# Token lists from one-hot products, and routed weights split one stage earlier

## The reference, cut to what matters

```python
shared_out = einsum('nh,dh->nd', silu(x_flat @ sw1.T) * (x_flat @ sw3.T), sw2)   # hidden 1024
s = sigmoid(x_flat @ router_w.T + t_bias)                    # 8 scores per token
_, topk_idx = top_k(s + router_bias, 2)                      # two experts per token
gates = s_sel / (denom + EPS)
H = gelu(einsum('nd,ehd->enh', x_flat, rw1))                 # hidden 256, every expert
O = einsum('enh,edh->end', H, rw2)
out = (shared_out + einsum('end,ne->nd', O, combine)) / 3
```

## Time and profile before

| | |
|---|---|
| median of three runs | 2856.93 us |
| the profiled execution | 2873.89 us, its span 2872.2 us |
| PE busy | 2552.8 us (89%) |
| DVE, ACT, POOL busy | 1227.9, 1012.8, 649.8 us |
| mean granted PE clock | 0.949 |
| shared stage | to about 722 us |
| routed stage | 722 to 1106 us |

### The profile page before, as it was taken

One profiled execution on the slowest core, in us unless ns is written; L12 is line 12 of the kernel. 1 busy time (PEld: TensorE's weight loads), 2 busy tenths in 40 slices (PEclk: granted clock), 3 DMA queues, 4 the chain that ended last, 5 costly groups with the idle time before them and its releaser, 6 DMA issues. The chain is left out here.

```text
span 2872.2 us, 43064 instructions
## 1 busy us (share of the span) xinstructions
PE 2552.8 (89%) x12487; PEld 2091.2 (73%) x12488; DVE 1227.9 (43%) x1642; ACT 1012.8 (35%) x1582; POOL 649.8 (23%) x572
## 2 busy tenths in 40 slices
PE   5776699999778784899899897799997999999999
PEld 1565578887666663788788786799996888888876
DVE  4412233333666663344343342566663333333346
ACT  3112233332766673222122221566664222222223
POOL 0223300000222221666566564000001111111100
PEclk9887899999898996999999999899998999999999
DMA  6899966665446344433633631666663111111125
GB/s 235 139 161 159 189 208 223 230 222 208 147 139 190 110 120 165 145 112 113 226 105 113 231 106 66 247 234 228 233 239 131 34 32 29 29 29 29 30 80 168
DMA packets 147234, 419.02 MB, mean 146 GB/s; under 512 B 42866, under 2 KB 45362, under 8 KB 130928
## 3 DMA queue, kind: packets, MB, share of 16 engines
q1 hardware_dynamic: 117872, 308.25, 35.0%
q0 software_dynamic: 21968, 69.27, 9.2%
q10 hardware_dynamic: 7344, 40.90, 4.0%
HBM read 593.35 MB, written 144.87 MB: 257 GB/s over the span
## 5 line engine op out<-in xcount | busy, mean ns | idle before, releaser
L646 POOL DMA_INDIRECT s_x<-in_x_rows,s_idx x72 | 91.6, 1272 | 645.3 <-DMA s_idx<-mid_slot_token 614.5
L87 PE MATMUL s_g<-wx_hi,s_x_hi 128*128 128x512 f32 x512 | 206.5, 403 | 6.9 <-DVE s_x_lo L1649 4.4
L89 PE MATMUL s_g<-wx_hi,s_x_lo 128*128 128x512 f32 x512 | 201.8, 394 | 0.0
L88 PE MATMUL s_g<-wx_lo,s_x_hi 128*128 128x512 f32 x512 | 201.1, 393 | 0.0
L1383 DVE TENSOR_TENSOR s_w_lo<-s_w_raw,s_w_hi 128x1024 fp32r<-128x1024 f32 x128 | 151.0, 1222 | 68.0 <-ACT s_w_hi L1335 66.4
L87 PE MATMUL s_g<-s_w_hi,s_c_hi 128*128 128x512 f32 x384 | 152.4, 397 | 0.0
L87 PE MATMUL s_h_ps<-s_x_hi,s_w_hi 128*128 128x256 f32 x512 | 145.6, 284 | 6.4 <-DVE s_w_lo L1383 6.4
L89 PE MATMUL s_g<-s_w_hi,s_c_lo 128*128 128x512 f32 x384 | 149.7, 390 | 0.0
L88 PE MATMUL s_g<-s_w_lo,s_c_hi 128*128 128x512 f32 x384 | 149.3, 389 | 0.0
L88 PE MATMUL s_h_ps<-s_x_lo,s_w_hi 128*128 128x256 f32 x512 | 145.5, 284 | 0.0
L89 PE MATMUL s_h_ps<-s_x_hi,s_w_lo 128*128 128x256 f32 x512 | 145.4, 284 | 0.0
(11 more groups left out here) (315 smaller groups left out, 7097.7 us busy)
## 6 DMA issues: line engine op xcount, KB each, us to landing
s_half<-mid_w ACTq DMA_DIRECT2D x128, 2048.0 KB
s_w_raw<-in_rw SPq DMA_DIRECT2D x144, 512.0 KB
s_w_raw<-in_w SPq DMA_DIRECT2D x64, 512.0 KB
mid_w<-s_x_grp SPq DMA_DIRECT2D x32, 1024.0 KB
mid_w<-s_pool_b SPq DMA_DIRECT2D x32, 1024.0 KB
s_w_raw<-in_w1h SPq DMA_DIRECT2D x16, 2048.0 KB, 8.1
s_w_raw<-in_w2h SPq DMA_DIRECT2D x16, 2048.0 KB, 7.7
mid_routed<-s_o_sb SPq DMA_DIRECT2D x72, 256.0 KB, 2.9
```

What stands on the lines that cost most here:

```text
L87: pe.matmul(out, a_hi, w_hi, start=first, stop=False, skip_group_check=True)
L88: pe.matmul(out, a_hi, w_lo, start=False, stop=False, skip_group_check=True)
L89: return pe.matmul(out, a_lo, w_hi, start=False, stop=last, skip_group_check=True)
L646: pool.indirect_dma_start(x[:, n], None, ins["x_rows"], bass.IndirectOffsetOnAxis(idx[:, n].bitcast(U32), 0)).then_inc(S[f"x_in{n}"], 16)
```

## The change

- Shared stage: the token lists are built by products. For every tile and each of its two experts DVE makes a one-hot matrix (token by lane within a list tile, `in_tile`) and a matrix (token by list tile, `tile_of`) that holds the token's lane number and tile number where it belongs; PE multiplies them, 8 matmuls per group (`list_tokens`), and DVE adds the sums over the groups (`add_list`). One instruction at the end makes token numbers of them, which stay in SBUF. The scatters and the clearing of `slot_token` are gone; the zero rows of `hash_in` now wait for the output tiles one by one.
- Shared stage: the parts are ten per expert, the first two being the routed weights of this expert (`d["rw"]`). They stand at chunks 1 to 7 and output tiles 0, 1 and 2.
- Routed stage: split weights of all eight experts have their place in SBUF (`w`, 128 KB per partition). SP loads an expert's weights whole, both parts, when the tile is the first of its expert, up to eight tiles ahead; the splits per tile are gone. PE reads the slot with two value loads per tile. The gather takes its indices from SBUF; POOL's program is unrolled over the 72 tiles. The loops of the other engines are unrolled by 8 (before, 4; DVE 2). The square weights `wo_raw` have one buffer and are split at tiles 1 and 12.

The diff, cut to its core:

```diff
     with ExitStack() as ctx:
...
-        NPART = 2 * DC
-        PART_CHUNKS, PART_OUT = (1, 2, 4, 5, 7, 8), (1, 2)
+        PARTS = [("rw", 0), ("rw", 1)] + [(w, k) for w in ("w1", "w2") for k in range(DC)]
+        NPART = len(PARTS)
+        PART_CHUNKS, PART_OUT = (1, 2, 3, 4, 5, 6, 7), (0, 1, 2)
...
             def raw_part(e, j):
-                sp.dma_start(w_raw[:, j % 2], ins["w1" if j < DC else "w2"][e, :, j % DC]
-                             ).then_inc(S[f"part_in{j % 2}"], 16)
+                name, k = PARTS[j]
+                src = ins["rw"][e, :, k * HS:(k + 1) * HS] if name == "rw" else ins[name][e, :, k]
+                sp.dma_start(w_raw[:, j % 2], src).then_inc(S[f"part_in{j % 2}"], 16)
+
+            def store_part(e, j):
+                name, k = PARTS[j]
+                dst = d["rw"][ER + e, :, k] if name == "rw" else d["w"][e * 2 + (name == "w2"), :, k]
+                sp.dma_start(dst, part[j % 2]).then_inc(S[f"part_out{j % 2}"], 16)
...
             for i in range(NB):
-                k = i % 2
-                wait_for(pool, S[f"tokens_sent{k}"], i // 2 * 32)
-                for c in (SLOT1, SLOT2):
-                    pool.indirect_dma_start(
-                        d["slot_token"], bass.IndirectOffsetOnAxis(rec[:, i, c:c + 1].bitcast(U32), 0),
-                        rec[:, i, TOKEN:TOKEN + 1], None).then_inc(S[f"tokens_sent{k}"], 16)
+                pool.wait_ge(S["mm2"], i + 1)
                 pool.dma_start(d["hash_in"][i * P:(i + 1) * P], zero[:]).then_inc(S["zero_out"], 16)
...
+            for c in range(2):
+                op(dve.tensor_scalar(hid, rec[:, :, SLOT1 + c], 7, None, ALU.arith_shift_right))
+                op(dve.tensor_copy(place[:, c, 0], hid))
+                op(dve.tensor_scalar(hid, rec[:, :, SLOT1 + c], P - 1, None, ALU.bitwise_and))
+                op(dve.tensor_copy(place[:, c, 1], hid))
+            op(dve.tensor_copy(lane[:], token_no[:, 0:1]))
+            op(dve.tensor_tensor_scan(iota[:], ones[:], ones[:], -1.0, ALU.mult, ALU.add))
+
+            def one_hots(g, n):
+
+                if n == 0:
+                    wait_for(dve, S["list_ps"], g)
+                i = g * TG + n
+                for c in range(2):
+                    tile, row = place[:, c, 0, i:i + 1], place[:, c, 1, i:i + 1]
+                    dve.tensor_scalar(in_tile[:, 2 * n + c], iota[:], row, None, ALU.is_equal).then_inc(S["one_hot"], 1)
+                    dve.tensor_scalar(tile_of[:, 2 * n + c, 0], tile_no[:, :, 0], tile, lane[:], ALU.is_equal,
+                                      ALU.mult).then_inc(S["one_hot"], 1)
+                    dve.tensor_scalar(tile_of[:, 2 * n + c, 1], tile_no[:, :, 0], tile, float(i), ALU.is_equal,
+                                      ALU.mult).then_inc(S["one_hot"], 1)
+
+            def add_list(g):
+                dve.wait_ge(S["list_ps"], g + 1)
+                if g == 0:
+                    dve.tensor_copy(token_list[:], list_ps).then_inc(S["list_sum"], 1)
+                else:
+                    dve.wait_ge(S["list_sum"], g)
+                    dve.tensor_tensor(token_list[:], token_list[:], list_ps, ALU.add).then_inc(S["list_sum"], 1)
+
+            def chunks(g):
+                for c in range(HC + 1):
+                    if c < HC:
+                        dve.wait_ge(S["silu"], g * HC + c + 1)
+                        wait_for(dve, S["h_lo"], g * HC + c - 1)
+                        dve.tensor_tensor(h[:, c % 2], sg[:, c % 2], up_ps[c % NG][:], ALU.mult).then_inc(S["hmul"], 1)
+                    if c > 0:
+                        dve.wait_ge(S["h_hi"], g * HC + c)
+                        dve.tensor_tensor(ht_lo[:, c - 1], h[:, (c - 1) % 2], ht_hi[:, c - 1],
+                                          ALU.subtract).then_inc(S["h_lo"], 1)
+                    if c in PART_CHUNKS:
+                        part_lo(g, PART_CHUNKS.index(c))
+                    if 2 <= c < 2 + TG:
+                        one_hots(g, c - 2)
+
             split_units(NU // 2 - 1)
...
-            software_pipeline(dve, G, [(1, chunks), (0, but_first(x_lo)), (1, late_parts)])
-
+            for g in range(G):
+                chunks(g)
+                add_list(g)
+                if g + 1 < G:
+                    x_lo(g + 1)
+                late_parts(g)
+
+            dve.wait_ge(S["list_sum"], G)
+            op(dve.scalar_tensor_tensor(keep["route"][:, 0], token_list[:, 1], float(P), token_list[:, 0], ALU.mult, ALU.add))
             op(dve.tensor_tensor(tile_ge, tile_no[:], end[:, None, :].to_broadcast([P, RT, ER]), ALU.is_ge))
...
-            op(dve.tensor_tensor(new[:, 2:RT], te[:, 2:RT], te[:, 0:RT - 2], ALU.not_equal))
-            op(dve.tensor_copy(keep["route"][:, 0], te))
-            op(dve.tensor_copy(keep["route"][:, 1], new))
+            op(dve.tensor_tensor(new[:, 1:RT], te[:, 1:RT], te[:, 0:RT - 1], ALU.not_equal))
+            op(dve.scalar_tensor_tensor(expert, new[0:1], float(ER), te[0:1], ALU.mult, ALU.add))
+            op(dve.memset(te, 1.0))
+            op(dve.tensor_tensor_scan(used, te, new, -1.0, ALU.mult, ALU.add))
+            op(dve.tensor_copy(slot, used[0:1]))
...
+            def list_tokens(g):
+
+                pe.wait_ge(S["one_hot"], (g + 1) * NPAIR * 3)
+                wait_for(pe, S["o_ready"], g * TG)
+                for n in range(NPAIR):
+                    mm = pe.matmul(aux_ps[:, 0:2 * RT], in_tile[:, n], tile_of[:, n].rearrange("p v t -> p (v t)"),
+                                   start=(n == 0), stop=(n == NPAIR - 1))
+                mm.then_inc(S["list_ps"], 1)
+
             def down(g):
                 if isinstance(g, int) and g == 0:
                     pe.wait_ge(S["w_lo"], NU)
                 for m in range(TG):
+                    if m == 1:
+                        pe.wait_ge(S["list_sum"], g + 1)
...
-                                      (0, down)])
+                                      (0, list_tokens), (0, down)])
...
+        w = sb("w", [P, ER, 2, 2, HS], FP32R)
...
+        def slot(eng, i):
+            return eng.value_load(slots[0:1, bass.ds(i, 1)], min_val=0, max_val=ER - 1)
+
         @block.sync
         def _(sp):
-            def load_idx(i, n, turn):
-                wait_for(sp, S[f"x_in{n}"], turn * 16)
-                sp.dma_start(idx[:, n], d["slot_token"][bass.ds(i * P, P)]).then_inc(S[f"idx_in{n}"], 16)
-
-            def load_w(name, c):
-                def stage(i, n, turn):
-                    expert = sp.value_load(route[0:1, 0, bass.ds(i, 1)], min_val=0, max_val=ER - 1)
-                    new = sp.value_load(route[0:1, 1, bass.ds(i, 1)], min_val=0, max_val=1)
-                    wait_apart(sp, S[name + "_lo"], i - 1)
-                    sp.dma_start(w_raw[:, n % 2, c], ins["rw"][expert, :, c],
-                                 cond=new > 0).then_inc(S[f"{name}_in{n % 2}"], 16)
-                return stage
+            def load_w(i, n, turn):
+                row = sp.value_load(experts[0:1, bass.ds(i, 1)], min_val=0, max_val=2 * ER - 1)
+                s = slot(sp, i)
+                wait_apart(sp, S["mm1"], i - 2 * NI + 1)
+                sp.dma_start(w[:, bass.ds(s, 1)].bitcast(FP32), d["rw"][bass.ds(row, 1)].rearrange("o p l s n -> p o l s n"),
+                             cond=row > ER - 1).then_inc(S[f"w_in{n}"], 16)
 
...
-            software_pipeline(sp, RT, [(0, load_idx), (2, load_w("w1", slice(0, W1))),
-                                       (3, load_w("w2", slice(W1, W1 + W2))), (4, load_wo), (7, store)], NI)
+                if isinstance(i, int) and i in WO_AT:
+                    m = WO_AT.index(i)
+                    wait_for(sp, S["wo_lo"], m)
+                    sp.dma_start(wo_raw[:], ins["square"][m]).then_inc(S[f"wo_in{m}"], 16)
+
+            software_pipeline(sp, RT, [(0, load_w), (2 * NI, store), (3, load_wo)], 2 * NI)
...
-            def gather(i, n, turn):
-                pool.wait_ge(S[f"idx_in{n}"], turn * 16 + 16)
-                wait_apart(pool, S["tx"], i - NI + 1)
-                pool.indirect_dma_start(x[:, n], None, ins["x_rows"],
-                                        bass.IndirectOffsetOnAxis(idx[:, n].bitcast(U32), 0)
-                                        ).then_inc(S[f"x_in{n}"], 16)
-
-            software_pipeline(pool, RT, [(0, gather)], NI)
+            for i in range(RT):
+                wait_for(pool, S["tx"], i - NI + 1)
+                pool.indirect_dma_start(x[:, i % NI], None, ins["x_rows"],
+                                        bass.IndirectOffsetOnAxis(idx[:, i:i + 1].bitcast(U32), 0)
+                                        ).then_inc(S[f"x_in{i % NI}"], 16)
 
...
-            def w1_lo(i, n, turn):
-                dve.wait_ge(S["w1_hi"], i + 1)
-                dve.tensor_tensor(w_lo[:, n, 0:W1], w_raw[:, n, 0:W1], w_hi[:, n, 0:W1],
-                                  ALU.subtract).then_inc(S["w1_lo"], 1)
-
...
```

(68 more changed lines are left out.)

79 lines of the change are left out of this document (27 added, 52 removed).

## The result

The changed kernel takes 2702.82 us (median of 4 runs, 2701.87 to 2703.94), beside 2854.06 us for the kernel before, timed together with it: a ratio of 0.9475, 95% interval 0.9452 to 0.9498. The prediction was 2699 us. The two stages behind the change only moved: from the first transfer of the stage after the routed one to the end it is 2701.5 - 932.1 = 1769.4 us, before it was 2872.2 - 1106.0 = 1766.2 us. So all of the gain lies ahead of that.

The account below looks back on a forecast made before the run. Scatters clogging the DMA engines bound the shared stage, SyncE's value loads the routed stage. Gains 89 + 69 = 158 us took the profiled 2873.9 to 2716 us, less 17 us for the median: 2699 us, range 2650 to 2778.

Parts of the forecast that it names:

- The cause in the shared stage: Shared stage, 102 to 400 us: 64 scatters clog the DMA engines, raw weights come late, and TensorE loses 106 us.
- The end of the shared stage, 628 us: Shared stage's last matmul: 66.9 + 537.4 + 4.4 + 2.3 + 7 + 10 = 628 us, against 717 us before.
- Ten small VectorE instructions, 2.3 us: Shared stage, before the first group's chunks: ten more small VectorE instructions put 2.3 us on the path.
- The gain of the shared stage, 89 us: Shared stage: ends at 628 instead of 717 us, a gain of 89 us, bounds 10 and 100.
- The pace of the routed stage, SyncE's sequencer: Routed stage before: four value loads per tile on SyncE fill the round of 4.91 us; TensorE needs 3.62 us.
- The price of a load, 0.98 us: Routed stage, SyncE: one value load with its register work costs about 0.98 us.
- "a quarter exposed": Routed stage, TensorE: a quarter of its two value loads' 1.96 us adds to 3.62 us, giving 4.1 us per tile.
- rival of mostly exposed loads: Routed stage: TensorE's value loads mostly exposed, 5.2 us per tile, a loss of 9 us, total 2777 us; chance 12%.
- feed-forward row: Feed-forward stage trace: TensorE makes two loads between matmuls of different tiles without wider gaps, taken as evidence for hidden loads.
- The head, 15.5 us from the stage's start: Routed stage to first output copy: 15.5 us, before 19.8; the 2 MB weight load replaces the 2.7 us index load.
- fifth rival: Shared stage: low rate comes from part stores beside zero rows, 192 GB/s, stage ends at 854 us, total 2925 us; chance 3%.
- Case 2: Value loads wholly hidden, parts never wait: routed 3.6 us per tile, gain 105 us, shared gain 99, total 2653 us; chance 20%.

Follow-up runs that it names:

- second profile of before: The kernel before, unchanged, profiled a second time: 2849.3 us, against 2873.9 us for the profiled execution that the prediction was made from.
- Loading by layer: Kernel with 9 TensorE value loads per 8 tiles, the first tile's routed weights fetched as two 1 MB transfers, one per layer: 2686.01 us, 0.942.
- twelve parts: Changed kernel with the two routed-weight parts loaded, split and stored twice, 12 parts per group instead of 10: 2715.22 us, 0.9519.
- 9 loads per 8 tiles: Changed kernel keeping the up-projection's slot register for the down-projection, 9 TensorE value loads per 8 tiles instead of 16: 2690.87 us, 0.9433.

## Why the prediction was right, step by step

**The cause in the shared stage: right.** Scatters out of the old kernel and its zero rows late: 87 us faster; 63 us of it are the scatters alone, once the zero rows are late. Scatters into the new one: 104 us slower. The waits had the shape that the chain said: raw weights late, ScalarE and VectorE behind them, TensorE last. What the step left out is that the zero rows between the scatters have a share of their own in it (24 us).

**The end of the shared stage, 628 us: 622.4 us.** The terms against the rows:
- Ten small VectorE instructions, 2.3 us: too small. In the first stretch TensorE issues 114 matmuls instead of the 131 of the earlier trace rows, and 135 in the kernel without scatters: (131 - 114) x 0.233 = 4 us. Another 2 us go in one wait of TensorE for VectorE that ends at 127 us (2.4 us, shown above). How much of the 6 us is these ten instructions and how much the first one-hots is not told apart.
- 64 list matmuls at 0.11 us, 7 us: too large. Eight start at 599.25 us, and the next matmul at 599.72 us:
```profile
599.25 0.67 PE L601 MATMUL s_aux<-s_scratch,s_oh 128*128 128x144 bf16 x8
599.72 0.48 PE L87 MATMUL s_first<-s_w_hi,s_ht_hi 128*128 128x512 f32 x1
```
  That is 0.06 us each, 3.8 us for all. The nearest row was a full-precision transpose, whose price per column is another.
- One-hots, 0.2 us each: 0.27 to 0.35 us, so about 1.8 us a chunk, and still hidden.
- Waits for parts, 10 us: TensorE has no lost time from 237 to 610 us; what is left of this term is 3 us at most.

**The gain of the shared stage, 89 us: 68 us of a typical run.** The end was right and the start of the comparison wrong. The sum says that the profiled execution "was 17 us slower than the median of the runs" and takes 17 us off its end, as if the excess would be there afterwards too. It lay in the crowded part, just what the change takes away, so it should have come off the gain and not off the end: 158 - 17 = 141 us, and 2716 us for the changed kernel.

**The pace of the routed stage, SyncE's sequencer: right.** In the second profile of before SyncE waits 0.2 us in all, from 745 to 1000 us; two loads fewer gain 75 us, two more cost 67 us. **The price of a load, 0.98 us: wrong**, it is 0.44 us by two loads more and 0.52 us by two fewer. The step divided the 1.98 us between two of SyncE's issues by its two value loads, and so put on them the conditional transfer's own register work (0.2 us in the median row of its line) and a longer first load. The profile before has rows for the loads themselves, 268 and 275 ns on SyncE in the median, which the prediction did not look up.

**Value loads on TensorE "a quarter exposed", 4.1 us per tile: 3.94 us.** Taking out 0.875 loads gave 0.17 us, so the two loads cost about 0.4 us per tile if the rest are exposed as much (an estimate), against the 0.48 us that the step added to 3.62 us; its reason (a price of 0.98 us, a quarter of it) was wrong in both factors, 0.55 us and a third, and the two errors cancel: that the term is good is luck. The rival of mostly exposed loads, 5.2 us per tile, is near what doubling them gives (5.05 us). This shows how far the feed-forward row carries: in the routed stage the queued matmuls hide about two thirds of the two loads that are there, and nothing of two more.

**The head, 15.5 us from the stage's start: about 20 us** (from the last shared copy 26.6 us, 24.9 before). The weights of the first tile were issued at 630.98 us and its up product started at 639.96 us, 9 us for 2 MB with 1.2 MB of gathers beside them. The term counted the 2 MB as no longer than the index load they replace. Loading by layer gives back 3.7 us of it. The 4 us put down for the two splits of the square weights do not show as a cost of their own; they lie within the mean of 3.94 us.

**The rivals.** The DMA engines do not bind at 240 GB/s: they gave 290 in the changed kernel and 328 with twelve parts. The fifth rival put the low rate down to part stores beside zero rows. The zero rows have 24 us of it, but without scatters the transfers run at 249 and 290 GB/s, far above the 210 at which that rival turns slower. Case 2 (2653 us) would have needed 3.6 us per tile; even with 9 loads per 8 tiles it is 3.77.

**The total, 2699 us: 2702.8 us, and in part by luck.** Against the second profile of before, the shared stage's gain was 21 us too high, the tiles gave 83 instead of 69 us, the square weights' 4 us fell away, and the head got longer by 1.7 us, not shorter by 4.3: 158 - 21 + 14 + 4 - 6 = 149 us. Without the misplaced 17 us the forecast would have been 2716 us, 13 us off instead of 4. The forecast of the total was better than that of its parts.

**What the prediction missed altogether** is that the change has two halves that bind at different places, and that its largest piece, resident weights, does nothing for the time. One value load fewer per weight stage gives nearly all of the routed gain (75 us, where the tiles of the changed kernel give 83). The tiles with splits then take 3.9 to 4.1 us, and those with resident weights, whose TensorE has loads of its own, 3.94. The change swapped one 4 us limit for another.

## What to carry to other kernels

When a queue's sequencer sets the pace, count its register work instruction by instruction, and take it out there (pack two values into one load, keep a register over the loop body) before moving data about. Scattering single words costs the transfers that run beside it; a few matmuls, with one-hots on an engine that has time to spare, are nearly free (here 3.8 us of TensorE and some 6 us before the first group, in place of 64 scatters). If the profiled run is off the median, find the stage with the excess, and ask whether the change takes it away, before using it as the start of a gain.

## What the runs showed of the hardware

- 64 scatters of 128 four-byte entries, paced two blocks at a time, move the last copy of the shared stage by 55 us in the kernel before with its zero rows late, by 81 us together with zero rows in their midst, and by 102 us in the busier stage of the changed kernel. Their packets take 1.1% of the engines' time from 102 to 237 us; the time per MB of the queue with most bytes (q1) there goes from 2.1% to 4.4%.
- A value load takes 0.27 us on SyncE (0.38 us for the slot in the changed kernel) and 0.30 us on TensorE in the median. With its check and register work one more costs 0.44 us on SyncE and 0.55 us on TensorE. The rule weighed in the prediction, a floor of about 600 ns ("DMA: Bandwidth & Descriptors", section "Latency and other measured facts", of the Trainium skill), is not what these loads from SBUF show; it is near what a load costs TensorE with all its work.
- A matmul of 144 columns of bf16 takes TensorE 0.06 us from start to start (eight in 0.47 us) at the full clock of 2.4 GHz.
